# A two-layer vision tower on one core: rounded split weights for the small expert works, and idle products in two waits of the heads

## The reference, cut to what matters

```python
# layer 0: a shared expert for every token, plus the 2 of 8 routed ones that the gate picks
def _expert(xf, W1, W2, W3):                     # W1, W3: 192 x 768, W2: 768 x 192
    gate = jnp.minimum(xf @ W1, LIMIT)
    up = jnp.clip(xf @ W3, -LIMIT, LIMIT)
    return jax.nn.silu(gate) * up @ W2
...
# layer 1, per head h of 16 numbers: out[l] = q[l] . (running, weighted sums of k v^T up to l),
# then a normalization of each head's output and
return out.reshape(B, L, D) @ Wo.T
```

## Time and profile before

| | |
|---|---|
| median of 3 runs | 531.9 us (530.1 to 535.51) |
| the profiled execution | 532.85 us |
| its span | 531.0 us, mean granted TensorE clock 0.987 |
| TensorE matmul busy | 489.6 us, 92% of the span |
| weight loads of TensorE busy | 463.7 us, 87% |
| VectorE busy | 352.2 us, 66% |
| ScalarE busy | 223.2 us, 42% |
| GpSimd busy | 179.0 us, 34% |
| small works' gate and up products (L776) | 432 matmuls, 49.7 us |

### The profile page before, as it was taken

How to read it: one execution, slowest core, us unless ns; L and a number is a source line. 1 busy time by engine, 2 the same in 40 slices (tenths; PEclk the granted TensorE clock), 3 DMA queues, 4 the chain that set the end, 5 groups by cost and what they waited for, 6 DMA issues and landing times.

```text
span 531.0 us, 9396 instructions
## 1 busy us (share of the span) xinstructions
PE 489.6 (92%) x3394; PEld 463.7 (87%) x3394; DVE 352.2 (66%) x859; ACT 223.2 (42%) x488; POOL 179.0 (34%) x161
## 2 busy tenths in 40 slices
PE   7899878988999999999999989997787889999995
PEld 6898878988999999999998879785665879999995
DVE  1674868864554565466454957999978674666665
ACT  0347573133343244244332237964832354344431
POOL 1502202741352553553452015786742100032200
PEclk9999999999999999999999989999998799999999
DMA  8760000567768578667834140000202000000001
GB/s 329 262 248 0 2 1 16 182 239 251 240 255 303 200 259 334 236 207 317 303 111 148 54 164 1 2 0 2 83 2 81 0 1 1 1 1 1 0 15 54
DMA packets 20974, 65.14 MB, mean 123 GB/s; under 512 B 5504, under 2 KB 13072, under 8 KB 17984
## 3 DMA queue, kind: packets, MB, share of 16 engines
q1 hardware_dynamic: 18864, 60.30, 31.6%
q0 software_dynamic: 2064, 4.24, 2.2%
HBM read 56.74 MB, written 7.79 MB: 122 GB/s over the span
## 4 chain that ended last, share of the span: by engine, by line
PE 54%; DVE 14%; DMA 6%; issue 3%; ACT 2%; POOL 2%; SPq 1%; DVEq 0%; POOLq 0%
PE psum L537 11%; PE psum L776 9%; PE psum L756 8%; PE psum L802 8%; DMA XR<-marked_rows 4%; PE psum L554 3%; PE psum L1201 3%; PE psum L1216 2%; PE psum L1233 2%; DVE AT L2228 2%; PE psum L1258 2%; POOL marked_rows L1606 2%; PE psum L561 2%; DVE H L2096 1%; DVE OW L2211 1%
## 5 line engine op out<-in xcount | busy, mean ns | idle before, releaser
L884 DVE TENSOR_SCALAR a0t<-psum 128x256 f32<-128x256 f32 (+1 forms) x93 | 41.8, 450 | 46.2 <-PE psum L776 26.6
L802 PE MATMUL psum<-w0d,a0h 128*128 128x192 f32 x408 | 69.7, 326 | 1.3 <-DVE a0h L891 1.3
L862 ACT ACTIVATE psum<-psum 128x256 f32<-128x256 f32 x75 | 27.5, 367 | 95.1 <-PE psum L776 55.0
L802 PEld LDWEIGHTS psum<-w0d,a0h 128*128 128x128 f32 x408 | 66.0, 190 | 1.6 <-DVE a0h L891 1.6
L852 POOL TENSOR_TENSOR w0l<-stage,w0h 128x768 fp32r<-128x768 f32 x18 | 32.9, 1826 | 74.2 <-DMA homes<-YO,XR 35.2
L537 PE MATMUL psum<-X,w1h 128*128 128x384 f32 x144 | 49.8, 346 | 1.6 <-DVE a1hf L692 1.6
L776 PE MATMUL psum<-XL,stage 128*128 128x128 f32 x432 | 49.7, 275 | 0.0
L776 PEld LDWEIGHTS psum<-XL,stage 128*128 128x128 f32 x432 | 49.4, 192 | 0.0
L1617 POOL DMA_INDIRECT homes<-YO,XR x25 | 24.2, 967 | 45.5 <-DVE YO L924 43.6
L632 ACT ACTIVATE a1s<-psum 128x384 f32<-128x384 f32 x36 | 17.6, 491 | 52.0 <-PE psum L537 52.0
L891 DVE SCALAR_TENSOR_TENSOR a0h<-psum,a0t 128x256 f32<-128x256 f32 x75 | 31.9, 425 | 9.9 <-ACT psum L862 1.7
(11 more groups left out here) (305 smaller groups left out, 1271.0 us busy)
## 6 DMA issues: line engine op xcount, KB each, us to landing
stage<-moe0w SPq DMA_DIRECT2D x19, 1536.0 KB, 8.0
w0d<-moe0d SPq DMA_DIRECT2D x19, 576.0 KB, 5.0
stage<-moe1w SPq DMA_DIRECT2D x4, 1056.0 KB, 4.9
marked_rows<-zero SPq DMA_DIRECT2D x3, 868.5 KB, 12.2
patch<-patches SPq DMA_DIRECT2D x3, 768.0 KB, 8.8
G<-homes SPq DMA_DIRECT2D x6, 288.0 KB, 4.8
XR<-marked_rows SPq DMA_DIRECT2D x8, 192.0 KB, 6.7
patch<-patches SPq DMA_DIRECT2D x3, 384.0 KB, 5.3
```

The source lines that it names most:

```text
L802: last = nc.tensor.matmul(dst, h, W0[par]["down"][:, fc, :], start=(fc == these[0]), stop=(fc == these[-1]))
L862: nc.scalar.activation(e_silu(fc, width, routed), bank[gate_bank(fc, routed)][:, 0:width], ACT.Silu).then_inc(S0["silu_ready"], 1)
L884: nc.vector.tensor_scalar(A0["t"][side][:, 0:width], bank[2 + side][:, 0:width], LIMIT, -LIMIT, ALU.min, ALU.max).then_inc(S0["clip_ready" ...
```

## The change

1. Small works 3, 5, ..., 17 take their gate and up weights split into high, low and second-half parts (`LW`), like the wide ones, and their rows split too (`XLh`, `XLl`): five float32r matmuls of 128 columns in the place of four float32 ones. Work 1 keeps its float32 products, from a buffer of its own (`first`).
2. The splits for work n+2 are made behind small work n: `e_lone_act` (four copies on ScalarE, behind `e_rows_high(n + 1)`) and `e_lone_low` (four subtractions on VectorE, behind `e_rows_low(n + 1)` and ahead of `e_copy(n - 1)`).
3. The rows of a small work get a low part as well: `e_rows_low` now stands behind every work, and TensorE waits for it (`x_lo`).
4. SP fetches the small weights earlier in the rotation: work 3's ahead of the loop, work n+4's at the end of turn n, waiting for the splits of work n+2 (`lw_lo`) and no longer for TensorE.
5. Twenty idle products ahead of `head_out(6)` and eighteen ahead of `transposes(3, 0)`.

```diff
@@ -207,7 +207,7 @@
         rt = [sb(f"rt{i}", [P, TILES * E0]) for i in range(6)]
-        rk = [sb(f"rk{i}", [P, TILES * E0 * E0]) for i in range(2)]
+        rk = [sb(f"rk{i}", [P, max(2 * LONE * E0, TILES * E0, TILES * E1 * E1)]) for i in range(2)]
         scan = [sb(f"scan{i}", [P, PAD + TILES * E0]) for i in range(3)]
@@ -248,6 +248,7 @@
             XL = sb("XL", [P, 2 * WT], F32, r1a)
+            XLh, XLl = (sb(name, [P, 2 * WT], F32R, r1a) for name in ("XLh", "XLl"))
                 patch = sb("patch", [P, PATCH_K * TOK], F32, s)
@@ -268,6 +269,9 @@
                     Y2 = sb("Y2", [P, TILES, XW1], F32, g)
+                    with ExitStack() as f:
+                        first = sb("first", [P, 4, F0], F32, f)
+                    LW = {k: sb(f"lw{k}", [P, 2, F0], F32R, g) for k in "hlt"}
             QK = sb("QK", [GW, GROUPS, QKVG], F32, r1b)
@@ -321,6 +325,7 @@
         marked, copied, numbered = sem("marked"), sem("copied"), sem("numbered")
+        lw_hi, lw_lo, ld_first = sem("lw_hi"), sem("lw_lo"), sem("ld_first")
         x_T, x_hi, x_lo, y_done, xl_first = (sem(s) for s in ("x_T", "x_hi", "x_lo", "y_done", "xl_first"))
@@ -377,7 +382,11 @@
         def staged(n):
-            return 16 * ((n + 1) // 2 + 1) if n % 2 else 16 * (n // 2 + 2)
+            return 16 * ((n + 1) // 2) if n % 2 else 16 * (n // 2 + 2)
+        def lone_split(n):
+            return 4 * ((n - 1) // 2)
         def low_engines(n):
@@ -447,14 +456,15 @@
                     wait_lows(sp, n - 2)
-                elif n > 1:
-                    sp.wait_ge(S["gu_ready"], units(n - 1))
+                elif n > 3:
+                    sp.wait_ge(lw_lo, lone_split(n - 2))
                 experts[n] = sp.value_load(eid[0:1, 1 - n % 2, (n - 1) // 2:(n - 1) // 2 + 1], min_val=1, max_val=E0)
-                sp.dma_start(flat[n % 2], moe0w[bass.ds(experts[n], 1)].rearrange(
-                    "e p c -> (e p) c")).then_inc(ld_stage[n % 2], 16)
+                to, loaded_to = (first.rearrange("p i f -> p (i f)"), ld_first) if n == 1 else (flat[n % 2],
+                                                                                                ld_stage[n % 2])
+                sp.dma_start(to, moe0w[bass.ds(experts[n], 1)].rearrange("e p c -> (e p) c")).then_inc(loaded_to, 16)
                 if n >= 2:
@@ -483,16 +493,18 @@
             load_rows(2)
+            load_weights(3)
                     if n + 2 <= WORKS:
-                        load_weights(n + 2)
                 load_down(n + 1)
+                if n % 2 and n + 4 <= WORKS:
+                    load_weights(n + 4)
             for c in range(CH):
@@ -737,7 +749,7 @@
                 if c is None:
-                    pe.wait_ge(x_lo, n // 2)
+                    pe.wait_ge(x_lo, n - 1)
                 if c is not None:
@@ -758,10 +770,13 @@
         def e_rows_gate_up(pe, u, n):
-            pe.wait_ge(xl_first, (n + 1) // 2)
-            pe.wait_ge(x_hi, n)
-            pe.wait_ge(ld_stage[1], staged(n))
-            w = W0[1]["stage"]
+            if n == 1:
+                pe.wait_ge(xl_first, 1)
+                pe.wait_ge(x_hi, 1)
+                pe.wait_ge(ld_first, 16)
+            else:
+                pe.wait_ge(x_lo, n - 1)
+                pe.wait_ge(lw_lo, lone_split(n))
                     pe.wait_ge(S0["silu_ready"], u + (g - 1))
@@ -772,9 +787,16 @@
                         cols = slice((2 * g + k) * P, (2 * g + k + 1) * P)
-                        for two in range(2):
-                            last = nc.tensor.matmul(dst[:, k * WT:(k + 1) * WT], w[:, 2 * mat + two, cols],
-                                                    XL[:, two * WT:(two + 1) * WT], start=(two == 0), stop=(two == 1))
+                        one, two = slice(0, WT), slice(WT, 2 * WT)
+                        if n == 1:
+                            ts = [(first[:, 2 * mat, cols], XL[:, one]), (first[:, 2 * mat + 1, cols], XL[:, two])]
+                        else:
+                            h, l, t = (LW[key][:, mat, cols] for key in "hlt")
+                            ts = [(h, XLh[:, one]), (l, XLh[:, one]), (h, XLl[:, one]), (t, XLh[:, two]),
+                                  (t, XLl[:, two])]
+                        for i, (wt, x) in enumerate(ts):
+                            last = nc.tensor.matmul(dst[:, k * WT:(k + 1) * WT], wt, x, start=(i == 0),
+                                                    stop=(i == len(ts) - 1))
         def e_down(pe, u, qpar, n, par, shared, ready, these=range(MOE0.fc)):
@@ -812,10 +834,10 @@
                 pe.wait_ge(S0["acc_done"], 3)
-            elif n % 2:
-                pe.wait_ge(x_lo, n // 2)
+            elif n == 2:
+                pe.wait_ge(x_hi, 1)
             else:
-                pe.wait_ge(x_hi, n - 1)
+                pe.wait_ge(x_lo, n - 2)
                 for t in range(tiles):
@@ -832,6 +854,28 @@
                                  ACT.Copy).then_inc(S0["w_hi"], 1)
+        def e_lone_act(act, n):
+            act.wait_ge(ld_stage[1], staged(n))
+            act.wait_ge(S0["gu_ready"], units(n - 1))
+            for i in range(4):
+                nc.scalar.activation(LW["t" if i % 2 else "h"][:, i // 2, :], W0[1]["stage"][:, i, :],
+                                     ACT.Copy).then_inc(lw_hi, 1)
+        def e_lone_low(dve, n):
+            for i in range(4):
+                dve.wait_ge(lw_hi, lone_split(n - 2) + i + 1)
+                if lone_split(n - 2) + i:
+                    dve.wait_ge(lw_lo, lone_split(n - 2) + i)
+                src, mat = W0[1]["stage"][:, i, :], i // 2
+                if i % 2:
+                    dst = LW["t"][64:P, mat, :]
+                    nc.vector.tensor_tensor(dst, src[64:P], dst.bitcast(F32), ALU.subtract).then_inc(lw_lo, 1)
+                else:
+                    nc.vector.tensor_tensor(LW["l"][:, mat, :], src, LW["h"][:, mat, :].bitcast(F32),
+                                            ALU.subtract).then_inc(lw_lo, 1)
         def e_split_low(engine, eng, n):
@@ -869,7 +913,9 @@
                 act.wait_ge(S0["gu_ready"], used)
-            if n % 2:
+            if n % 2 and n > 1:
+                nc.scalar.activation(XLh[:], bank[6][:, 0:2 * WT], ACT.Copy).then_inc(x_hi, 1)
+            elif n % 2:
             else:
@@ -907,7 +953,8 @@
             dve.wait_ge(x_hi, n)
-            nc.vector.tensor_tensor(XWl[:], bank[6][:, 0:4 * WT], XWh[:].bitcast(F32), ALU.subtract).then_inc(x_lo, 1)
+            to, of, cols = (XLl, XLh, 2 * WT) if n % 2 else (XWl, XWh, 4 * WT)
+            nc.vector.tensor_tensor(to[:], bank[6][:, 0:cols], of[:].bitcast(F32), ALU.subtract).then_inc(x_lo, 1)
         def e_acc(dve, t0, t1, at, ready):
@@ -1272,10 +1319,14 @@
                 for i in outs[2:]:
+                    if i == 6:
+                        pe.wait_ge(l1_Tc, (HH + 1) * GROUPS)
+                        keep(0, 20)
             head_O(GROUPS - 1)
+            keep(0, 18)
             for i in range(8, 14):
@@ -1430,6 +1481,7 @@
                         e_rows_high(act, n + 1, units(n))
+                        e_lone_act(act, n + 2)
                     for fc in range(1, FC0):
@@ -2077,8 +2129,10 @@
                     e_dve(dve, u, 0, 2 * WT, downs(n - 2))
+                if n < WORKS:
+                    e_rows_low(dve, n + 1)
                 if n % 2 and n < WORKS:
-                    e_rows_low(dve, n + 1)
+                    e_lone_low(dve, n + 2)
                 if n > 1:
```

## The result

| | before | after |
|---|---|---|
| median of the runs | 531.75 us (n = 4) | 550.24 us (545.67 to 552.69, n = 4) |
| ratio | | 1.033, 95% interval 1.027 to 1.039 |
| profiled execution | 532.85 us | 545.67 us |
| its span, mean granted clock | 531.0 us, 0.987 | 543.9 us, 0.994 |
| routed stage, first rows' transpose to the end of work 17's products | 164.8 us | 183.3 us |

The prediction of 550 us came true. All of the loss lies in the routed stage, +18.5 us; the profiled execution lost less (12.8 us) because 4.3 us came back behind the stage and 1.4 ahead of it (0.6 of these 1.4 is a shorter wait for work 1's rows: 1.0 us in place of 1.6).

The account below looks back on a forecast made before the run. TensorE was taken to bound the routed works. Terms 10.4 + 7.7 + 2.4 - 0.7 - 1.4 = +18.4 on 532.85 us give 551.3; with the median 0.95 lower, 550 us was predicted, range 537 to 561.

Parts of the forecast that it names:

- Products, +10.4 us: Small works' gate and up products: 60 matmuls at 111 ns, 6.66 us, 1.30 more in each of eight works.
- Rivals 1 and 2: Small works' matmul pace: columns set it, 525 us, chance 0.05; or 0.09 us holds for 128-column weights, 540 us, 0.05.
- Waits for the clip, +7.7 us: Wide works behind small works 3 to 15: TensorE waits 1.1 us for VectorE's clip queued behind the splits, seven times.
- Rival 3: VectorE's burst of splits is hidden and TensorE never waits for the clip: 540 us, chance 0.08.
- The lag is worked off and no second wait follows: Wide works: VectorE needs two instructions of some 0.42 us a step, TensorE 1.14, so TensorE waits only once.
- First turn, +2.4: Work 2, behind work 1: no down product covers the splits, so TensorE waits 2.4 us for the clip.
- The chain behind `e_copy`, 0: Result copies, sends, GpSimd's splits and stage 0: delay and use move together, 2 to 3 us against 2.4; costed at nothing.
- Rival 4: Stage 0 lands late, the chain behind `e_copy` slipping another microsecond or two a turn: 8 us more, 558 us, chance 0.08.
- Row waits, -0.7: SP's queue: row fetches no longer stand behind the small weights, so waits for rows shrink by 0.7 us.
- Idle products, -1.4: Heads: filling the first wait brings the eight score matmuls to full clock, -1.4 us; the second filling counted at nothing.
- Rival 5, the clock: Clock falls in the small works, 1.4 us lost each turn: 11 us more, 561 us, longer falls 570; chance 0.10.

Follow-up runs that it names:

- split_columns: After, with each product of small works 3 to 17 made as two of 64 columns (120 matmuls, not 60): 681.31 us, one run, beside 544.46 for before.
- half_weights_first: After, with 60 added matmuls in each small work 3 to 17, using the left 64 weight columns: 590.22 us, one run, beside 544.46 for before.
- no_burst: After, with the small weights split only once, for work 3, and the other seven bursts of copies and subtractions left out: 542.07 us, ratio to before 1.016.
- burst_only: Before, plus four copies on ScalarE and four subtractions on VectorE behind each small work, results unused, 48 matmuls kept: 543.18 us, ratio to before 1.020.
- spread_splits: After, with VectorE's four subtractions taken apart among the result copies, the fourth behind step 2 of the wide work: ratio to before 1.029, stage 193.4 us.
- spread_later: After, with VectorE's four subtractions taken apart among the result copies, the fourth behind step 3 of the wide work: ratio to before 1.026, stage 191.2 us.
- no_idle: After, without its twenty and eighteen idle products in the heads: 551.84 us, ratio to before 1.036.
- pool_halves3: After, with the two half-height subtractions of each small work's split moved from VectorE to GpSimd: ratio to before 1.036, stage 199.9 us.

## Why the prediction was right, step by step

- **Products, +10.4 us.** Right: 6.65 us for 60, 1.29 more in each of eight works, 10.3. The reason was right too, as `split_columns` and `half_weights_first` show together. Rivals 1 and 2 fell with it.
- **Waits for the clip, +7.7 us.** Right in place, too large in size: 0.74 us a turn where 1.1 was forecast, about 5.2 in all, within the stated 0.6 to 1.6 a turn. (After less `no_burst` gives 7.0, but about 2 of that is late landings.) The wait's own row is 0.48 us in a plain turn, not 1.0, and costs about 0.65 to 0.75, since the row counts from the end of the last product's passage, 0.28 us behind its start, where the pace is 0.11. The splits went 1.06 us apart as in the earlier trace rows; but the copies of the result took 0.62 for the two, and the clip followed within 0.54. Rival 3 (hidden) is refuted by both `burst_only` and `no_burst`.
- **"The lag is worked off and no second wait follows".** Right for after: a lagging step takes 0.86 us against TensorE's 1.14, and in the plain turn above there is one wait. The second waits in three wide works come with a late stage 0 (next but one below). But the margin is small. `spread_splits` and `spread_later` moved the wait to the sixth step and to the next small work instead of ending it.
- **First turn, +2.4.** Measured +2.30, with a wait of 2.2 us. It was not always so cheap: in the profiles of `burst_only` and `no_idle` 3.4 us at half clock follow on that wait, and the first turn takes 20.51 and 20.38 us in place of 18.78.
- **The chain behind `e_copy`, 0.** This term was put too low: about 2 us. Stage 0 lands late in some turns of after (ScalarE waits 9.8 us in six, against 1.5 in two), and in `burst_only` one turn lost 2.2 us to it and some 1.6 more to the half clock behind. Rival 4 is thus real, at a quarter of its size, and inside the 7.0. That the clip was 2.5 us below its term and this 2 above its own, so that the sum of both came out, is luck. The argument that use and delay move together holds on the average, but a slack of zero leaves nothing for a transfer that takes 6.7 us here and 7.9 there.
- **Row waits, -0.7.** Right. Three times in before's stage the first transpose of a work's rows starts 0.30 to 0.35 us behind the product ahead of it, in place of 0.12: 0.6 us, and after has none of them. (The wait for work 1's rows lies ahead of the stage.) The stage but for the seven bursts came to 11.5, where products and first turn make 12.6: 1.1 us less, of which these are 0.6. Wide works that take 6.82 us, and not 7.07 as in some of before's turns, are a part of the rest; why they do stays open.
- **Idle products, -1.4.** The pair gave 2.7 (interval 1.2 to 4.1), inside the bounds and nearly twice the term. Its make-up was wrong: the first filling, which was counted, gives nothing alone, and the second, counted at nothing, is needed.
- **Rival 5, the clock.** No fall in after's small works, nor in those of any other run with 128 columns a load. With half the columns a load, in `split_columns`, the clock falls in each of them.

Of the whole: the stage was forecast at +19.8 and came to +18.5 in the profile. Less the 2.7 us of the idle products that would make +15.8, but the medians differ by 18.5. With some 3 us of interval on either side of after's ratio the difference can't be told, and that the median came out at 550.24, as near as that to 550, is luck too.

## What to carry to other kernels

Where a matmul has 128 four-byte weight columns and 128 or 64 moving columns, count matmuls, not columns or passes: 5 one-pass products in place of 4 passes are 25% more. A split that has to be remade each turn is a burst on another engine: add up that engine's list between two uses, with each instruction at the length it has beside its neighbours; where little is left, another order only moves the wait. Idle products in one of two waits gave nothing here that could be measured, in both 0.5%: try them alone and as a set.

## What the runs showed of the hardware

- The pace of these matmuls is that of the weight load: 0.11 us with 128 weight columns and 128 or 64 moving ones, 0.06 with 64 weight columns (`split_columns`, `half_weights_first`). At half clock it is 0.21 us in place of 0.11, so a load-bound stream takes nearly twice its time there.
- TensorE can be 100% busy by the profile, with loads back to back, and still lose its clock: in `split_columns` it did in every small work from 3 on (64 columns a load), in after in none (128).
- A wait of 2.2 us in work 2 was followed by 3.4 us at half clock in two profiled executions (`burst_only`, `no_idle`) and by none in two others (after, `no_burst`).
- A wait costs more than its own row, by about 0.2 us, where the products before it start 0.11 us apart (0.48 us in the row, 0.65 between the starts, in after).
- Two-input subtractions of VectorE and GpSimd side by side: 2.00 to 2.54 us in place of 0.96 on VectorE (`pool_halves3`, `spread_later`, `spread_splits`), 4.34 for two in place of twice 1.82 on GpSimd; the earlier trace rows had shown 1.50 for one.
